# GpSimd takes over the wait for landed additions, the expert tiles lie in two lists, and rectified rows are made between two exponentials

## The chip, the cores and the metric

The kernel runs on one core of one Trainium2 chip. The metric is the device time of one execution in microseconds (us), median of several runs; lower is better. TensorE (PE in the profile) does matrix products and transposes, VectorE (DVE) and ScalarE (ACT) do the elementwise work, GpSimd (POOL) issues the indirect DMAs, SyncE (SP) issues the plain ones.

## What is computed

Three layers over 6250 nodes of 256 features: graph attention (`gnn`), a linear-attention block (`mix`), and a mixture of six experts (`ffn`), of which each node takes two. The change lies wholly in the last of them:

```python
xn = _layernorm(x, axis=-1)
x = x + _L0_gnn_ref(xn, ...) + _L0_mix_ref(xn[None], ...)[0]
x = x + _L0_ffn_ref(_layernorm(x, axis=-1)[None], ...)[0]

def _L0_ffn_ref(features, ...):
    rh = jax.nn.relu(features @ router_w1 + router_b1)
    expert_logits = jax.nn.softmax(rh @ router_w2 + router_b2, axis=-1)
    top_w, top_i = jax.lax.top_k(expert_logits, TOP_K)        # TOP_K = 2, six experts
    routing_weights = jax.nn.softmax(top_w, axis=-1)
    h1 = jax.nn.relu(jnp.einsum('bsd,edh->bseh', features, expert_w1) + expert_b1)
    h2 = jax.nn.relu(jnp.einsum('bseh,ehf->bsef', h1, expert_w2) + expert_b2)
    expert_out = jnp.einsum('bsef,efo->bseo', h2, expert_w3) + expert_b3
    sel = jnp.take_along_axis(expert_out, top_i[:, :, :, None], axis=2)
    return jnp.sum(sel * routing_weights[..., None], axis=2)
```

## The kernel before

Everything below happens in the last block of the kernel, from about 1740 us of the span on. Each engine has its own instruction stream, in program order; semaphores tie them together.

**Router stage.** The 50 row tiles of 125 nodes are taken in `NS` = 5 groups of `SIZES` = (6, 10, 10, 12, 12). For group g, ScalarE makes the normalised rows (`features`, line 2219), TensorE transposes them and runs the router (lines 2303, 2313, 2322) with ScalarE copying in between, and VectorE's `route(g)` takes the logits (line 2074), asks ScalarE for an exponential (line 2276, waits for `d_lm`), picks the two best experts, and after the instruction of line 2088 asks for a second exponential (line 2278, waits for `d_dd`). VectorE doesn't wait for this second one at once: it first counts ranks and comes to it at line 2100 (`a_ee`). ScalarE, though, stands at line 2278 till `d_dd` comes. Only then it makes the rectified attention rows of group g + 2 (`relus`, line 2208), and then goes to `features(g + 1)`. With `route(g)` done (`d_pos`), GpSimd writes each row of the group twice, once into the region of either expert in the DRAM tensor `moe_rows` (line 1951, two indirect DMAs for a row tile, 100 in all).

**List of tiles.** `MT` = 54 tiles of 256 rows are worked through, each with rows of one expert. `table_of(0)` (after group 3's counts) lists the first `FULL` = 20 of them, from the full tiles that the first `EARLY` = 3 groups give each expert. `table_of(1)`, called by VectorE after its tile step 1, lists tiles 20 to 53: the rest of the first list (full tiles of the early groups, expert by expert), then a second list (the further full tiles, expert by expert), then a third (the partly filled tile of each expert). Each is a run of instructions on segments, `SEG` = 18 of them for three lists; the comparison of 34 tiles with 18 segments has 612 elements. From the list VectorE also makes `clear1` and `clear2`: for tile j the count that the semaphore `sent[...]` of tile j - 1 (j - 2) must have reached before tile j may be added. If both tiles belong to one expert no node is in both, and the count is one that was reached long ago; if the expert changed, it is the count that says that the earlier additions have landed in `out`.

**Tile loop.** For tile j SyncE loads the rows (line 1928), TensorE transposes them (line 2349, `row_turn`) and multiplies by three weight matrices (`up` line 2360, `mid` line 2371, `down` line 2384). Its order is up(j+1), mid(j), row_turn(j+2), down(j-1). ScalarE copies and rectifies (lines 2239, 2247, 2256). VectorE's order in its step j is stage1(j+2), stage2(j+1) (copies of the expert's weights and biases), weighed(j-1), stage3(j): the products of tile j - 1 are scaled into the buffer `yo` (line 2171, two halves), then the third weight matrix is copied (line 2145), which `down(j)` needs. `yo` has three buffers, so weighed(j) also waits till the additions of tile j - 3 have landed. Before that `weighed` reads `clear1` and `clear2` from memory into registers (line 2161) and waits on `sent[...]` (this is the wait that moves). GpSimd issues two indirect DMAs a tile that add the rows of `yo` to `out` (line 1971), and in tiles 0 to 8 also the two writes of one more row tile of the last group (line 1951; three of its twelve row tiles were written ahead).

At tile 20 SyncE first fills the ends of the six regions with a blank (line 1919) and waits for it before it loads on.

Of the kernel before, what the change touches and what calls it, by code (L numbers as in the profile page):

```python
# [18 lines left out]
ALU = mybir.AluOpType  # L19
# [114 lines left out]
def gps_kernel(nc, x, src, dst, gW, gWb, ga, gab, Wq, bq, Wk, bk, Wv, bv, Wo, bo, W1, b1, W2, b2,  # L134
# [7 lines left out]
    with ExitStack() as ctx:  # L142
# [1656 lines left out]
        odd6 = take(NX)  # L1799
        SEG = 3 * NX  # L1800
        fulls = take(SEG + NX)
        seg_n, seg_end, seg_off = take(SEG), take(SEG), take(SEG)
        seg_step = take(3, NX)
        cmp_mem = take((MT - FULL) * SEG)
# [88 lines left out]
        with nc.Block() as block:  # L1893
# [37 lines left out]
            def _(g_):  # L1931
                last_node = g_.to_reg(N - 1)
                g_.memset(blank[:, 0:MW - 2], 0.0)
                g_.memset(blank[:, MW - 2:MW - 1].bitcast(I32), N)
# [32 lines left out]
                g_.wait_ge(base_out, 16 * NS)  # L1967
                for j in range(MT):
                    g_.wait_ge(d_y, 2 * j + 2)
                    for s in range(2):  # L1970
                        g_.indirect_dma_start(out=out, out_offset=bass.IndirectOffsetOnAxis(ap=node[:, j % RING3, s:s + 1], axis=0),  # L1971
                                              in_=yo[:, j % 3, s, :], in_offset=None, bounds_check=last_node, oob_is_err=False,
                                              compute_op=ALU.add).then_inc(sent[j % PB3], 16)
                    if AHEAD_OF_ADDS + j < SIZES[g]:
                        write(g, AHEAD_OF_ADDS + j, sent_late)
# [4 lines left out]
            def _(dve):  # L1980
# [13 lines left out]
                dve.wait_ge(z3, 4)  # L1994
                V.memset(seg_step[:, 2, NX - 1:NX], -float((NX - 1) * PACK) + float(PACK // 4)).then_inc(z3, 1)

# [37 lines left out]
                def table_of(k):  # L2034
# [14 lines left out]
                    if k == 1:  # L2049
                        step(V.scalar_tensor_tensor(odd6, whole, -float(MR), count, ALU.mult, ALU.add))  # L2050
                        step(V.scalar_tensor_tensor(fulls[:, SEG:SEG + NX], odd6, 1.0, whole, ALU.min, ALU.add))
                    V.tensor_tensor(seg_off[:, 0:n], fulls[:, 1:1 + n], fulls[:, NX:NX + n], ALU.subtract)
# [63 lines left out]
                regs = [dve.alloc_register(f"expert{i}") for i in range(4)]  # L2116
                clears = [dve.alloc_register(f"clear{i}") for i in range(4)]
                found = [dve.alloc_register(f"found{i}") for i in range(2)]

# [35 lines left out]
                def weighed(j):  # L2155
                    e = expert(j)
                    held = []
                    for back, clear in ((1, clear1), (2, clear2)):
                        if j >= back:
                            k, reg = (j - back) % PB3, clears[2 * (j % 2) + back - 1]  # L2160
                            dve.reg_load(found[back - 1], clear[0:1, j:j + 1])
                            dve.reg_alu(reg, found[back - 1], 0, ALU.max)
                            held.append((sent[k], dve.snap(reg, min_val=sent_rows[k], max_val=landed(j - back))))
                    for other, value in held:
                        dve.wait_ge(other, value)
                    dve.wait_ge(t_d, j + 1)
# [34 lines left out]
            def _(act):  # L2201
# [60 lines left out]
                for g in range(NS):  # L2262
# [12 lines left out]
                    act.wait_ge(d_lm, g + 1)  # L2275
                    A.activation(pe_[0:R, 0:n], lm[0:R, 0:n], ACT.Exp).then_inc(a_pe, 1)
                    act.wait_ge(d_dd, g + 1)
                    A.activation(ee[0:R, 0:n], dd[0:R, 0:n], ACT.Exp).then_inc(a_ee, 1)
                    if g + 2 < NS:
                        relus(g + 2)  # L2280
                row_turned(1)
# [162 lines left out]
```

## Time and profile before

| | us |
|---|---|
| three runs | 2219.26, 2229.14, 2229.53 |
| median | 2229.14 |
| the profiled execution: its time | 2220.27 |
| the profiled execution: its span | 2218.5 |
| TensorE busy in it | 1856.9 (84%) |
| VectorE busy | 1689.0 (76%) |
| ScalarE busy | 1441.6 (65%) |
| GpSimd busy | 1201.3 (54%) |
| router stage and tile loop | about 1740 to 2211 of the span |

A row of a timeline gives the start and the length of an instruction (or of a run of them) in us, its engine, line, operation and operands, and in brackets how long the engine had been idle before it and what ended this. "issue" is idle time that no recorded wait explains. PEclk is the granted clock of TensorE as a share of full speed.

### The profile page before, as it was taken

The numbers are of one execution on the slowest core, as the hardware profiler recorded it, in microseconds if no ns is written. First come the engines' busy times: TensorE is split into PE (matmuls) and PEld (weight loads), VectorE is DVE, ScalarE is ACT, GpSimd is POOL, SyncE is SP. The second block draws the span as 40 slices with busy tenths as digits, with TensorE's granted clock in tenths as the row PEclk, the third lists the DMA queues.
The fourth block names the chain that finished last, engine by engine and source line by source line (L and its number), as shares of the span: only waits on it lengthen the run. The fifth ranks groups of instructions, "written<-read, shape, count | busy, mean of one in ns | idle before, by whom it ended". The sixth has DMA issues, their size and how long they took to land. (4 is left out here: it accounts for less than half of the span.)

```text
span 2218.5 us, 49553 instructions
## 1 busy us (share of the span) xinstructions
PE 1856.9 (84%) x10024; PEld 1491.2 (67%) x10024; DVE 1689.0 (76%) x5423; ACT 1441.6 (65%) x4425; POOL 1201.3 (54%) x1164
## 2 busy tenths in 40 slices
PE   3888857599954999999999999999999556999995
PEld 2444435377743778877878778878877455778884
DVE  7898879877754788888888889888898655455553
ACT  5567558244412889889889889889889663333331
POOL 2010000056565777777777777777774167755553
PEclk9999979599856999999999999999999768999997
DMA  4322101021103444444443444444442454655551
GB/s 144 95 76 60 53 24 52 19 83 49 42 23 84 121 119 119 122 119 117 122 118 111 120 114 117 123 117 117 122 117 69 148 172 136 118 117 89 101 92 26
DMA packets 133895, 215.45 MB, mean 97 GB/s; under 512 B 42813, under 2 KB 89084, under 8 KB 133604
## 3 DMA queue, kind: packets, MB, share of 16 engines
q0 software_dynamic: 61920, 132.16, 24.9%
q1 hardware_dynamic: 67022, 72.68, 10.7%
q10 hardware_dynamic: 4662, 7.46, 1.1%
q8 instruction: 94, 1.54, 0.3%
q14 instruction: 197, 1.61, 0.2%
HBM read 150.28 MB, written 56.51 MB: 93 GB/s over the span
## 5 line engine op out<-in xcount | busy, mean ns | idle before, releaser
L1394 POOL DMA_INDIRECT area<-wh_table,area x788 | 769.9, 977 | 260.2 <-issue 235.0
L1721 PE MATMUL bank<-area 128*126 x1960 | 484.2, 390 | 31.0 <-ACT area L1641 15.3
L1721 PEld LDWEIGHTS bank<-area 128*126 128x126 f32 x1960 | 349.8, 188 | 103.8 <-issue 55.1
L1427 DVE TENSOR_SCALAR area<-iota_row,area 128x126 f32<-128x126 f32 x980 | 355.0, 369 | 24.5 <-ACT area L1594 17.3
L1627 ACT ACTIVATE area<-iota_row,area 128x126 f32<-128x126 f32 x735 | 285.8, 389 | 0.0
L1971 POOL DMA_INDIRECT out_dram<-area x108 | 171.2, 1585 | 134.3 <-DVE area L2171 115.7
L1641 ACT ACTIVATE area<-area 128x126 f32<-128x126 f32 x735 | 237.0, 386 | 0.4
L590 POOL DMA_INDIRECT sorted_slots<-area x112 | 134.9, 1204 | 115.9 <-DVE area L946 85.4
L1580 ACT ACTIVATE area<-bank 125x512 bf16<-125x512 f32 x245 | 145.4, 593 | 79.2 <-DVE area L1441 76.1
L1741 PE MATMUL bank<-area 128*128 128x250 f32 x800 | 189.1, 380 | 6.8 <-ACT area L1648 3.7
L1502 DVE SCALAR_TENSOR_TENSOR acc_mem<-acc_mem,area,bank 125x258 f32 x245 | 117.8, 481 | 97.0 <-PE bank L1709 82.4
L1752 PE MATMUL bank<-area 128*125 128x256 f32 x800 | 188.9, 379 | 0.0
L1697 PE MATMUL bank<-ident,area 128*126 128x128 f32 x980 | 158.1, 284 | 34.8 <-DVE area L1427 34.8
L1741 PEld LDWEIGHTS bank<-area 128*128 128x128 f32 x800 | 154.0, 193 | 27.0 <-ACT area L1648 4.1
L1441 DVE TENSOR_REDUCE area<-bank 125x1 f32<-125x512 f32 x245 | 167.5, 684 | 0.0
L1752 PEld LDWEIGHTS bank<-area 128*125 128x125 f32 x800 | 150.0, 187 | 23.0
L2171 DVE SCALAR_TENSOR_TENSOR area<-bank,area 128x256 f32<-128x256 f32 x108 | 47.5, 480 | 142.8 <-DMA out_dram<-area 74.0
L2247 ACT ACTIVATE area<-bank,area 128x256 f32<-128x256 f32 x108 | 45.3, 470 | 159.7 <-issue 147.2
L583 POOL IOTA acc_mem<- 128x788 f32 x1 | 0.8, 793 | 272.7 <-DVE area L855 272.7
L1951 POOL DMA_INDIRECT moe_rows<-acc_mem,area x100 | 100.4, 1004 | 67.2 <-issue 28.6
L1697 PEld LDWEIGHTS bank<-ident,area 128*126 128x126 f32 x980 | 103.9, 141 | 40.0 <-DVE area L1427 39.7
L2384 PE MATMUL bank<-area 128*128 128x256 f32 x432 | 108.1, 394 | 16.3 <-DVE area L2145 16.3
(417 smaller groups left out, 4050.4 us busy)
## 6 DMA issues: line engine op xcount, KB each, us to landing
area<-moe_rows SPq DMA_DIRECT2D x54, 264.0 KB, 2.9
area<-wh_table,area POOLq DMA_INDIRECT x788
area<-area SPq DMA_DIRECT2D x17, 388.5 KB
wh_table<-area SPq DMA_DIRECT2D x50, 126.5 KB
xn<-in_x_dram SPq DMA_DIRECT2D x25, 250.0 KB
xt_rows<-area SPq DMA_DIRECT2D x50, 125.0 KB, 2.5
area<-xt_rows SPq DMA_DIRECT2D x25, 250.0 KB
x_rows<-area SPq DMA_DIRECT2D x25, 250.0 KB
```

The lines of the kernel that those rows point to most:

```text
L590: g.indirect_dma_start(out=slots[k % 2].rearrange("(a b) -> a b", b=1), out_offset=bass.IndirectOffsetOnAxis(ap=dest[:, j, k:k + 1], axis= ...
L1394: g.indirect_dma_start(out=gath[:, (i + GT) % RS, :], out_offset=None, in_=table, in_offset=bass.IndirectOffsetOnAxis(ap=idx_tab[:, i:i + ...
L1427: ins = V.tensor_scalar(xm[:, b, t, :], iota_row[:, :], rowl[:, j % 10, t:t + 1], fetched(j, D)[:, t:t + 1], ALU.is_equal, ALU.mult)
L1441: V.tensor_reduce(gmax[0:R, b:b + 1], bank[XT[j % 2]][0:R, :], AX.X, ALU.max).then_inc(d_m, 1)
L1580: A.activation(hot[0:R, b, :], bank[XT[j % 2]][0:R, :], ACT.Sign).then_inc(a_hot, 1)
L1627: last = A.activation(dist[:, t, :], iota_row[:, :], ACT.Abs, bias=rowl[:, j % 10, t:t + 1], scale=-1.0)
L1641: last = A.activation(sm[:, b, t, :], dist[:, t, :], ACT.Exp, bias=e3[:, b, t:t + 1], scale=-1.0e12)
L1697: last = T.transpose(bank[XT[j % 2]][0:RW, t * L:(t + 1) * L], xm[:, b, t, :], ident[:, :])
L1721: last = T.matmul(bank[US[b]][0:RW, 0:WROW], sm[:, b, t, :], gath[:, bass.ds(place + t, 1), 0:WROW].rearrange("p a w -> p (a w)"), start=( ...
L1741: last = T.matmul(bank[HB[p % 2]][:, i * CH:(i + 1) * CH], w_1[:, k, f * 128:(f + 1) * 128], x1T[:, k, :], start=(k == 0), stop=(k == 1))
L1752: last = T.matmul(bank[AB][0:R, r * D:(r + 1) * D], hT[:, f, r * R:(r + 1) * R], w_2[:, f, :], start=(f == 0), stop=(f == 7))
L1971: g_.indirect_dma_start(out=out, out_offset=bass.IndirectOffsetOnAxis(ap=node[:, j % RING3, s:s + 1], axis=0), in_=yo[:, j % 3, s, :], in_ ...
```

## The change

1. The reads of `clear1` and `clear2` and the waits on `sent[...]` leave VectorE's `weighed`. GpSimd does them before it issues tile j's additions: it waits for `tabled`, reads both values, waits for `d_y` as before, then waits for the two counts.
2. The tiles from 20 on lie in two lists, not three: the second list has for each expert its further full tiles and its partly filled one (`whole` becomes the number of both). `SEG` is 12, the comparison has 408 elements. The number of tiles is the same.
3. ScalarE makes `relus(g + 2)` after the first exponential of group g and before it waits for the second one, for g = 0, 1, 2.

```diff
--- before.py
+++ after.py
@@ -1797,10 +1797,10 @@
         sel, seen, going = (a.rearrange("p (e t) -> p e t", e=NX) for a in (sel_mem, seen_mem, going_mem))
         blank_i, count_i = take(NX).bitcast(I32), take(NX).bitcast(I32)
         odd6 = take(NX)
-        SEG = 3 * NX
+        SEG = 2 * NX
         fulls = take(SEG + NX)
         seg_n, seg_end, seg_off = take(SEG), take(SEG), take(SEG)
-        seg_step = take(3, NX)
+        seg_step = take(2, NX)
         cmp_mem = take((MT - FULL) * SEG)
         ej_f, both_f = take(MT), take(MT)
         both_i = take(MT).bitcast(I32)
@@ -1930,6 +1930,8 @@
             @block.gpsimd
             def _(g_):
                 last_node = g_.to_reg(N - 1)
+                clears = [g_.alloc_register(f"clear{i}") for i in range(4)]
+                found = [g_.alloc_register(f"found{i}") for i in range(2)]
                 g_.memset(blank[:, 0:MW - 2], 0.0)
                 g_.memset(blank[:, MW - 2:MW - 1].bitcast(I32), N)
                 g_.memset(blank[:, MW - 1:MW], 0.0)
@@ -1966,7 +1968,17 @@
                     write(g, i, sent_late)
                 g_.wait_ge(base_out, 16 * NS)
                 for j in range(MT):
+                    g_.wait_ge(tabled, 1 if j < FULL else 2)
+                    landings = []
+                    for back, clear in ((1, clear1), (2, clear2)):
+                        if j >= back:
+                            k, reg = (j - back) % PB3, clears[2 * (j % 2) + back - 1]
+                            g_.reg_load(found[back - 1], clear[0:1, j:j + 1])
+                            g_.reg_alu(reg, found[back - 1], 0, ALU.max)
+                            landings.append((sent[k], g_.snap(reg, min_val=sent_rows[k], max_val=landed(j - back))))
                     g_.wait_ge(d_y, 2 * j + 2)
+                    for added, value in landings:
+                        g_.wait_ge(added, value)
                     for s in range(2):
                         g_.indirect_dma_start(out=out, out_offset=bass.IndirectOffsetOnAxis(ap=node[:, j % RING3, s:s + 1], axis=0),
                                               in_=yo[:, j % 3, s, :], in_offset=None, bounds_check=last_node, oob_is_err=False,
@@ -1992,7 +2004,7 @@
                 V.memset(going[0:R, :, 0:1], 0.0)
                 V.memset(seg_step[:, :, NX - 1:NX], -float((NX - 1) * (PACK + REG))).then_inc(z3, 1)
                 dve.wait_ge(z3, 4)
-                V.memset(seg_step[:, 2, NX - 1:NX], -float((NX - 1) * PACK) + float(PACK // 4)).then_inc(z3, 1)
+                V.memset(seg_step[:, 1, NX - 1:NX], -float((NX - 1) * PACK) + float(PACK // 4)).then_inc(z3, 1)
 
                 def residual(g):
                     for c in pairs[g]:
@@ -2048,7 +2060,7 @@
                     step(V.tensor_copy(whole, count_i))
                     if k == 1:
                         step(V.scalar_tensor_tensor(odd6, whole, -float(MR), count, ALU.mult, ALU.add))
-                        step(V.scalar_tensor_tensor(fulls[:, SEG:SEG + NX], odd6, 1.0, whole, ALU.min, ALU.add))
+                        step(V.scalar_tensor_tensor(whole, odd6, 1.0, whole, ALU.min, ALU.add))
                     V.tensor_tensor(seg_off[:, 0:n], fulls[:, 1:1 + n], fulls[:, NX:NX + n], ALU.subtract)
                     step(V.tensor_tensor(seg_n[:, 0:n], fulls[:, NX:NX + n], fulls[:, 0:n], ALU.subtract))
                     V.scalar_tensor_tensor(seg_off[:, 0:n], seg_off[:, 0:n], float(MR), step_n, ALU.mult, ALU.add)
@@ -2114,8 +2126,6 @@
                     V.tensor_copy(posi[0:R, :, f:f + n], posf3[0:R, :, 0:n]).then_inc(d_pos, 1)
 
                 regs = [dve.alloc_register(f"expert{i}") for i in range(4)]
-                clears = [dve.alloc_register(f"clear{i}") for i in range(4)]
-                found = [dve.alloc_register(f"found{i}") for i in range(2)]
 
                 def expert(j):
                     return dve.snap(regs[j % 4], min_val=0, max_val=NX - 1)
@@ -2154,15 +2164,6 @@
 
                 def weighed(j):
                     e = expert(j)
-                    held = []
-                    for back, clear in ((1, clear1), (2, clear2)):
-                        if j >= back:
-                            k, reg = (j - back) % PB3, clears[2 * (j % 2) + back - 1]
-                            dve.reg_load(found[back - 1], clear[0:1, j:j + 1])
-                            dve.reg_alu(reg, found[back - 1], 0, ALU.max)
-                            held.append((sent[k], dve.snap(reg, min_val=sent_rows[k], max_val=landed(j - back))))
-                    for other, value in held:
-                        dve.wait_ge(other, value)
                     dve.wait_ge(t_d, j + 1)
                     if j >= 3:
                         dve.wait_ge(sent[j % PB3], landed(j - PB3))
@@ -2274,10 +2275,10 @@
                         up(0)
                     act.wait_ge(d_lm, g + 1)
                     A.activation(pe_[0:R, 0:n], lm[0:R, 0:n], ACT.Exp).then_inc(a_pe, 1)
+                    if g + 2 < NS:
+                        relus(g + 2)
                     act.wait_ge(d_dd, g + 1)
                     A.activation(ee[0:R, 0:n], dd[0:R, 0:n], ACT.Exp).then_inc(a_ee, 1)
-                    if g + 2 < NS:
-                        relus(g + 2)
                 row_turned(1)
                 for j in range(MT):
                     if j + 1 < MT:
```

## Rows read from the trace of the kernel before

**Rows 1.** Engines by stretch: busy us (instructions), PEclk, DMA share, GB/s
```profile
2050.00:2100.00 50.00, 50.00 (x250) 43.72 (x249) 29.53 (x102) 18.83 (x45) 29.27 (x20) 1.00 0.58 99
```

**Rows 2.** Waits from 1900 us on: waiter <- releaser: us in total, times, longest
```profile
POOL out_dram L1971 <- DVE area L2171: 113.6, 45, 8.6
DVE area L2171 <- DMA out_dram<-area: 69.7, 22, 8.5
...
PE bank L2384 <- DVE area L2145: 16.3, 8, 4.3
...
PE bank L2349 <- DMA area<-moe_rows: 4.9, 1, 4.9
```

**Rows 3.** Chain that ended last, in order of time: start, us, what
```profile
2077.03 1.74 PE bank L2384 x8
...
2082.66 1.74 PE bank L2384 x8
...
2193.99 1.57 POOL out_dram L1971
2195.87 3.57 DMA out_dram<-area
```

**Rows 4.** Timeline of VectorE, line 2171 at tiles 1, 2, 8 and 13
```profile
1888.22 0.88 DVE L2171 SCALAR_TENSOR_TENSOR area<-bank,area 128x256 f32<-128x256 f32 x2 [0.79 <-DMA out_dram<-area]
...
1895.56 0.88 DVE L2171 SCALAR_TENSOR_TENSOR area<-bank,area 128x256 f32<-128x256 f32 x2 [3.57 <-DMA out_dram<-area]
...
1935.28 0.88 DVE L2171 SCALAR_TENSOR_TENSOR area<-bank,area 128x256 f32<-128x256 f32 x2 [8.49 <-DMA out_dram<-area]
...
1962.86 0.88 DVE L2171 SCALAR_TENSOR_TENSOR area<-bank,area 128x256 f32<-128x256 f32 x2 [1.86 <-PE bank L2384]
```

**Rows 5.** Timeline of TensorE, three places where it waited for VectorE (before down(9) and down(25), and at up(4))
```profile
1887.05 2.58 PE L2360 MATMUL bank<-area 128*128 128x256 f32 x8 [3.92 <-DVE area L2131]
...
1936.54 3.46 PE L2384 MATMUL bank<-area 128*128 128x256 f32 x8 [4.16 <-DVE area L2145]
...
2041.58 2.00 PE L2384 MATMUL bank<-area 128*128 128x256 f32 x8 [0.93 <-DVE area L2145]
```

**Rows 6.** Timeline of GpSimd: first write of group 3; first additions of tiles 0, 3, 7, 44, 53
```profile
1843.59 0.97 POOL L1951 DMA_INDIRECT moe_rows<-acc_mem,area  x1 [3.54 <-DVE area L2114]
...
1881.99 1.93 POOL L1971 DMA_INDIRECT out_dram<-area  x1 [0.30 <-issue]
...
1903.31 1.62 POOL L1971 DMA_INDIRECT out_dram<-area  x1 [0.30 <-issue]
...
1929.34 1.62 POOL L1971 DMA_INDIRECT out_dram<-area  x1 [0.32 <-issue]
...
2147.90 1.57 POOL L1971 DMA_INDIRECT out_dram<-area  x1 [2.21 <-DVE area L2171]
...
2207.43 1.55 POOL L1971 DMA_INDIRECT out_dram<-area  x1 [3.27 <-DVE area L2171]
```

**Rows 7.** Timeline of ScalarE: second exponential of groups 0 and 2, rectified rows of group 3
```profile
1758.42 0.21 ACT L2278 ACTIVATE area<-area 125x6 f32<-125x6 f32 x1 [2.50 <-DVE area L2088]
...
1782.36 4.88 ACT L2208 ACTIVATE acc_mem<-acc_mem,area 125x256 f32<-125x256 f32 x12
...
1806.55 0.21 ACT L2278 ACTIVATE area<-area 125x10 f32<-125x10 f32 x1 [2.80 <-DVE area L2088]
```

**Rows 8.** Timeline of VectorE: use of the second exponential; the comparison of either table
```profile
1784.04 0.17 DVE L2100 TENSOR_SCALAR area<-area 125x10 f32<-125x10 f32 x1
...
1838.92 0.28 DVE L2056 TENSOR_TENSOR area<-area 128x120 f32<-128x120 f32 x1
...
1881.64 0.80 DVE L2056 TENSOR_TENSOR area<-area 128x612 f32<-128x612 f32 x1
```

**Rows 9.** Register reads of line 2161: ns min/median/max, first and last start
```profile
L2161 DVEq TENSOR_LOAD <-area x105: 297/312/803, 1887.1 to 2201.9; - x105
```

**Rows 10.** Additions of line 1971, from the start of an issue to landing
```profile
DMA to landing us min/median/max: 2.7/3.9/5.0
```

## The prediction, made from the kernel before alone

> **What bounds the kernel now.** I first read the engines by stretch. In the middle of the tile loop TensorE is busy for all of 50 us, at its full granted clock, and no other engine for more than 30 [rows 1]. The chain of waits says the same: its products follow each other without a gap, and one tile takes 2082.66 - 2077.03 = 5.63 us, which I call the beat, 5.64 [rows 3]. So what a change can give lies where TensorE stands still. The list of waits has the places: GpSimd waits 113.6 us for VectorE and VectorE 69.7 us for landed additions, but TensorE itself waited for VectorE only 16.3 us in eight places [rows 2]. The difference is cover: after a late `weighed(j-1)` VectorE still has 2 to 3 us in hand before `down(j)` needs its copy. Of the 69.7 us most is therefore worth nothing. Uncovered are the wait before tile 8 (VectorE 8.49 us, TensorE 4.16) [rows 4, 5], two of about 1 us at tiles 25 and 26 (the first is in [rows 5]), and the end. There the last seven tiles (47 to 53) each have another expert than the one before: issue 1.57 us, gap, issue, landing 3.57, VectorE 0.9, issue [rows 3], 6.6 to 7 us a tile and not 5.64. Changes of expert can be counted by VectorE's waits for a DMA: tiles 1, 2, 8, 14, 22, 24, 25, 26, 32, 38, 45 and 47 to 53, 18 in all. In the first nine tiles GpSimd is a second bound: it has two writes beside each tile's two additions, never idles, and takes (1929.34 - 1903.31) / 4 = 6.51 us a tile [rows 6], more than the beat. In the router stage the bound is the round ScalarE, TensorE, ScalarE.
>
> **Rectified rows between the exponentials.** Before the second exponential of groups 0, 1 and 2 ScalarE idles 2.50 to 2.80 us (three waits, 8.0 together) [rows 7]. The rectified rows (4.88 us for twelve) now lie in this gap, so `features` of the next group starts earlier each time: 8.0 less about 0.15 a group for a later restart, 7.6 us for the round and for the first tile of the loop. The price: the second exponential comes about 5 us after the first. VectorE used it at 1784.04 in group 1 [rows 8]; it would be there at about 1784.5, 0.5 us late. VectorE has that to spare: at the end of each group it waits for ScalarE anyway. GpSimd gains less. Its writes of groups 1 and 2 run on without a gap, so it gains the first 2.4 less 0.5, and then the idle 3.54 before group 3 [rows 6] shrinks to 0.3: 1.9 + 3.2 = 5.1 us. Tile 0's additions start at 1876.9, not 1881.99.
>
> **Two lists.** Three instructions on 612 elements take 0.80 us each, on 120 elements 0.28 [rows 8]: 1.06 ns an element, 204 elements fewer, 0.65 us in all. TensorE waits for just this table (3.92 us before up(4)) [rows 5], so it is a gain. Changes of expert fall from 18 to 12: none in the last tiles but that of the filler tile 53. With the wait on GpSimd a change costs little: 1.87 us between the two issues, 3.9 from issue to landing [rows 10] and 0.15 make 5.9, against the beat of 5.64. By itself the second edit is worth 0.65 and some 2 to 4 us at the end.
>
> **The wait on GpSimd.** VectorE is freed. It waits for tile j - 3 only, so the 4.16 us at tile 8 go, and with them what the first products after it lost by a low clock (3.46 and not 1.90 us, 1.56) [rows 5]. TensorE is then up by 7.6 + 0.65 + 5.7 = 14.0 us at tile 9. What GpSimd takes on is r, a time per tile for two reads of memory into registers, two register operations and the extra waits; later tiles hide it, since GpSimd idles 2.21 us before an issue [rows 6], but tiles 1 to 9 don't. No read by GpSimd is in the trace. The nearest rows are VectorE's reads of the same words: 0.312 us median [rows 9], with the register operations 1.1 us when nothing covers them, which is the upper bound of the likely case; the lower is 0, if GpSimd's sequencer reads while the write before it (0.97 us) is still made. With a single read VectorE still stood 0.79 us [rows 4], so reads are covered in part at best; GpSimd's cover of 0.97 us is most of the 1.1, but its sequencer isn't seen to work ahead. I take 0.5, between the two. What is queued behind the new wait on GpSimd: the writes of the last group, which SyncE needs only at tile 20. At the changes 2 and 8 the two writes lie between the issue and the wait (1.6 + 2 x 1.28 + gaps = 4.5 us against 3.9), so nothing is added there.
>
> By the Trainium skill (Perfetto Trace Analysis, DMA Instruction — SWDGE) the sequencer is free to fetch on once such an instruction is in the wait queue. That would hide the reads; yet the rows show a gap of 0.30 us between any two of them, unexplained. By that rule the sum would be its r = 0 case.
>
> So GpSimd starts tile 9 at 1876.9 + 6.7 (tile 0) + 8 x 6.51 + 9r = 1935.7 + 9r (tile 0 as before: issues of 1.93 and 1.57, two writes, four gaps), tile 10 at 3.8 + r more: 1944.5 for r = 0.5. `yo` has three buffers, so `weighed(13)` can't start before 1944.5 + 5.9 = 1950.4. It started at 1962.86 [rows 4]: a gain of 12.4, less than TensorE's 14.0, and the smaller decides. From there the beat holds, as 3.8 + r is below 5.64.
>
> **The rest.** SyncE's load for tile 20 makes TensorE wait 4.9 us [rows 2]: SyncE can send the blanks only after tile 19's load, which waits for VectorE's tile 15, and that came some 1.5 us late as tile 14 was a change. I take 1.0 (0 to 1.5). Tiles 25 and 26: 2.0. End: tiles 44 to 53 took 2207.43 - 2147.90 = 59.5 [rows 6]. After: six beats 33.8, one without a transpose 5.2, one of GpSimd's own 3.8 + 0.5, and 5.9 for the filler tile: 49.2. Gain 10.3. What follows the last issue stays.
>
> Sum: 12.4 + 1.0 + 2.0 + 10.3 = 25.7. With r = 0: 14.0 + 1.5 + 2.0 + 10.8 = 28.3. With r = 1.1 `weighed(13)` comes at 1956.4, gain 6.5, and 6.5 + 0 + 2.0 + 9.7 = 18.2.
>
> **The rivals.**
> Dear reads, r from 1.2 to 1.9. For: between two DMA instructions GpSimd always shows a gap, so its sequencer may not work ahead. Against: VectorE's reads are 0.3. At r = 1.5 the gain at tile 13 is 2.5, at the end 9.3, with the 2.0 some 14: 2215.
> The Trainium skill (DMA: Bandwidth & Descriptors, Latency and other measured facts) gives such a load a floor of about 600 ns. VectorE's 312 ns don't agree; if GpSimd's did, two would be 1.2 us, by that an r of this rival.
>
> The start is eaten. The router stage begins earlier for TensorE, but GpSimd's issues or SyncE's loads keep their time. For: GpSimd gains only 5.1 of 7.6 in any case. Against: its 3.54 us gap is plain. With 7 us less the gain is 18 to 19: 2210.
>
> Slower: GpSimd becomes the bound of every tile. Its own work is 3.72 us a tile; above r = 1.92 it passes the beat. Its last tile then starts at 1876.9 + 6.7 + 52.1 + 44 x 3.72 + 53r = 2099.4 + 53r, which meets today's 2207.43 at r = 2.04. At r = 2.5 it is 24.5 us later: 2254. It would need reads three times as long as VectorE's.
>
> Nothing changes: freed time is lost to more transfers at once, landings rise from 3.9 us towards 5.0 [rows 10] and TensorE waits on `yo` or on row loads. A landing of 5.0 makes a change 7.0 us, still for 12 tiles only, and without changes three buffers allow three beats: under 10 us lost, so this takes more than one mishap. About 2226.
>
> **How the numbers follow.** The profiled execution had 2220.27; with 25.7 less it is 2194.6. The four executions lie at two levels, 2219 to 2220 and 2229, and the median of 2229.14 is of the upper, which gives 2203.4. I say 2199.0, between them. Chances: the forecast (r to 1.1) 0.68, with the gain from 18 to 28; dear reads 0.12, a third of it within 0.5%; start eaten 0.10; slower 0.05; nothing 0.05. From 2219 less 28 and the level's spread the range starts at 2187; above it takes in the smaller gains to 15 us from the upper level, 2214. A difference below 0.5%, 11 us, can't be told from none here. So faster 0.87, within 0.08, slower 0.05.
>
> **What would show it.** ScalarE's line 2278 without idle time in groups 0 to 2. GpSimd's gap before line 1971 in tiles 3 to 7: 0.30 + r; its beat there 7.0 us. VectorE's line 2171 with short DMA waits only in tiles 10 to 14. No wait of 4 us before down(9). Last tiles at 5.64. Wrong it would be if GpSimd's issues after tile 12 follow each other with no idle time, or if TensorE stands longer than before in front of up(4) or row_turn(20).

## The result, and the profile after

The changed kernel takes 2193.95 us (median of four executions, 2192.44 to 2203.05) against 2224.20 (four, 2218.12 to 2229.53). The ratio is 0.9879, with a 95% interval of 0.9847 to 0.9911. That is 27 us less (the two medians lie 30 us apart), and more than the 11 us below which the prediction would have called it no difference. The forecast was 2199.0, with a range from 2187 to 2214. The profiled execution had 2192.44 us with a span of 2190.5, 28.0 less than the span of before.

The page of the changed kernel: busy times, and the chain that ended last by engine.

```profile
PE 1854.1 (85%) x10024; PEld 1491.2 (68%) x10024; DVE 1690.2 (77%) x5423; ACT 1442.9 (66%) x4425; POOL 1202.5 (55%) x1164
...
PE 16%; issue 2%; DVE 1%; ACT 1%; DMA 0%; POOL 0%; SPq 0%; DVEq 0%; POOLq 0%; ACTq 0%
```

No engine's busy time changed by more than 2.8 us. What changed is who waits. Waits of the changed kernel from 1880 us on (waiter <- releaser: us in total, times, longest):

```profile
DVE area L2172 <- PE bank L2385: 112.9, 52, 7.2
POOL out_dram L1983 <- DVE area L2172: 80.7, 39, 7.2
POOL out_dram L1983 <- issue: 27.3, 62, 3.4
...
PE bank L2361 <- DVE area L2141: 4.1, 1, 4.1
...
POOL out_dram L1983 <- DMA out_dram<-area: 3.9, 5, 2.7
...
PE bank L2350 <- DMA area<-moe_rows: 3.3, 1, 3.3
...
PE bank L2385 <- DVE area L2155: 1.4, 1, 1.4
```

Against [rows 2]: VectorE's 69.7 us behind landed additions are gone. GpSimd waits for them in VectorE's place, with 3.9 us put down to a landing and part of the 27.3 us of "issue". TensorE's eight waits for the copies before `down` (line 2145 of before, 16.3 us) are one, at the very end. What stays are the table (4.1) and the load of tile 20 (3.3).

TensorE's timeline of the changed kernel has the three waits. Below it, from GpSimd's timeline, the first additions of tiles 44 and 53:

```profile
1879.66 3.78 PE L2361 MATMUL bank<-area 128*128 128x256 f32 x8 [4.15 <-DVE area L2141]
1973.47 1.12 PE L2350 MATMUL bank<-ident,area 128*128 128x128 f32 x4 [3.26 <-DMA area<-moe_rows]
2173.29 2.00 PE L2385 MATMUL bank<-area 128*128 128x256 f32 x8 [1.42 <-DVE area L2155]
```

```profile
2130.74 1.57 POOL L1983 DMA_INDIRECT out_dram<-area  x1 [2.21 <-DVE area L2172]
...
2179.77 1.55 POOL L1983 DMA_INDIRECT out_dram<-area  x1 [2.72 <-DMA out_dram<-area]
```

Tiles 44 to 53 take 49.03 us where they took 59.53 [rows 6].

For comparing many kernels one origin is needed. The code ahead of this block is the same in all, yet the block begins anywhere from 1737 to 1750 us of the span. So the table counts from the start of ScalarE's first normalised row of the block (line 2220 of the changed kernel, the column "block starts"). The next columns are starts of `weighed(j)` on VectorE, in us after that origin, and the end of the span, each from one profiled execution. Before and after begin together, so their difference of 28.1 is that of the spans.

| kernel | block starts | w(0) | w(3) | w(8) | w(13) | w(16) | w(17) | w(44) | w(53) | end |
|---|---|---|---|---|---|---|---|---|---|---|
| before | 1744.6 | 133.1 | 156.0 | 190.7 | 218.2 | 235.2 | 247.3 | 402.1 | 461.7 | 473.9 |
| changed | 1744.7 | 125.4 | 149.0 | 177.2 | 205.3 | 222.2 | 232.8 | 384.9 | 430.7 | 445.8 |
| wait_only | 1742.7 | 134.7 | 157.6 | 185.8 | 214.0 | 230.9 | 243.7 | 396.4 | 442.6 | 463.4 |
| lists_only | 1742.1 | 132.1 | 154.2 | 189.3 | 217.1 | 234.0 | 246.1 | 398.2 | 447.4 | 459.6 |
| relus_only | 1746.9 | 125.1 | 148.9 | 184.0 | 212.8 | 229.7 | 242.9 | 397.5 | 456.5 | 468.7 |
| no_lists | 1742.3 | 125.6 | 149.3 | 177.5 | 205.7 | 222.6 | 232.9 | 385.2 | 431.1 | 451.3 |
| no_wait_move | 1737.4 | 125.4 | 149.0 | 183.8 | 212.8 | 229.7 | 243.0 | 396.3 | 445.7 | 457.8 |
| reads12 | 1750.0 | 124.9 | 148.6 | 176.7 | 204.9 | 221.8 | 234.5 | 386.9 | 432.8 | 448.0 |
| reads3_live | 1746.6 | 125.2 | 147.2 | 175.4 | 203.5 | 220.4 | 231.7 | 384.4 | 430.3 | 445.2 |
| reads6_live | 1747.0 | 125.7 | 149.1 | 177.3 | 205.4 | 222.3 | 235.1 | 387.5 | 433.4 | 448.5 |
| blanks_early | 1750.4 | 125.9 | 148.0 | 176.1 | 204.3 | 221.2 | 226.8 | 378.9 | 424.7 | 440.0 |
| table_early | 1747.7 | 125.4 | 142.2 | 171.5 | 201.4 | 218.3 | 231.2 | 383.7 | 429.6 | 444.8 |
| both_early | 1749.7 | 125.3 | 142.1 | 171.2 | 201.2 | 218.2 | 223.8 | 375.9 | 421.7 | 436.8 |

The step from w(16) to w(17) holds TensorE's wait for the rows of tile 20. In the kernels that leave that load where it was it takes 10.3 to 13.3 us where a beat is 5.64. The changed kernel and its repeat (reads12) have 10.6 and 12.7, so some 2 us of this are no property of a kernel.

### The profile page after: what moved, and what is told of

Read it like the earlier page. It is cut to its first block and busy times, and to the rows that moved or that the text cites. A ratio compares the mean times of both kernels' runs of the same rounds, so it can differ in the third digit from the quotient of the medians.

```text
span 2190.5 us, 49554 instructions
## 1 busy us (share of the span) xinstructions
PE 1854.1 (85%) x10024; PEld 1491.2 (68%) x10024; DVE 1690.2 (77%) x5423; ACT 1442.9 (66%) x4425; POOL 1202.5 (55%) x1164
```

## The experiments

### Each part alone

Part 1 alone, GpSimd's wait (`weighed` on VectorE loses its reads and waits as in the change):

```diff
+                    g_.wait_ge(tabled, 1 if j < FULL else 2)
+                    # reads of clear1, clear2 as in the change
                     g_.wait_ge(d_y, 2 * j + 2)
+                    for added, value in landings:
+                        g_.wait_ge(added, value)
```

> Only the wait on landed additions moves to GpSimd; three lists and the late rectified rows stay. Theory (GpSimd's reads are covered by the write that is being made, and a change of expert costs GpSimd 5.9 us against a beat of 5.64): TensorE loses no 4.16 us before down(9), 1 us twice at tiles 25 and 26, and 1.5 us less at tile 20; the last seven tiles go at 5.9 each. 5.7 + 1.7 + 2 + 6.6 = 16 us, span 2202.5 against 2218.5. Rival 1 (the gain of the whole change comes from fewer changes of expert and the early rectified rows): under 5 us, span over 2213. Rival 2 (GpSimd's reads cost): its gap before line 1971's first issue in tiles 3 to 7 is 0.8 to 1.4 us and not 0.30.

Measured: ratio 0.9930 (0.9909 to 0.9950), median 2209.04. By the ratio that is 15.6 us (11 to 20), near the 16 expected. From the block's start its one profile ends at 463.4, 10.5 us before the kernel before. Its first tile came 1.6 us late, though nothing ahead of it is edited; without that it would be 12. The loop gained what was said: no wait before down(9), w(53) 19 us earlier. The last stretch gave some back. GpSimd's first additions in it:

```profile
2176.48 1.55 POOL L1983 DMA_INDIRECT out_dram<-area  x1 [3.21 <-issue]
...
2182.79 1.68 POOL L1983 DMA_INDIRECT out_dram<-area  x1 [2.89 <-DVE area L2172]
...
2189.21 1.55 POOL L1983 DMA_INDIRECT out_dram<-area  x1 [2.88 <-issue]
...
2195.37 1.55 POOL L1983 DMA_INDIRECT out_dram<-area  x1 [2.75 <-issue]
```

They are 6.2 to 6.4 us apart where every tile has another expert than the one before, not 5.9. Over tiles 44 to 53 that makes 2195.37 - 2140.25 = 55.1 us: better than 59.5, worse than the 49.0 that parts 1 and 2 give together. In tiles 45 and 47 to 53 of this run GpSimd's addition starts 0.74 us after the landing that it waited for. In the kernel before, with VectorE's two halves of `weighed` between them, it is 1.30 in the same tiles. So moving the wait saves 0.56 us of each such change.

Part 2 alone, two lists:

```diff
-        SEG = 3 * NX
+        SEG = 2 * NX
...
-                        step(V.scalar_tensor_tensor(fulls[:, SEG:SEG + NX], odd6, 1.0, whole, ALU.min, ALU.add))
+                        step(V.scalar_tensor_tensor(whole, odd6, 1.0, whole, ALU.min, ALU.add))
```

> Only two lists for three; VectorE still waits for landed additions. Theory: the end gains 9 us (six of seven changes of expert gone), tiles 25 and 26 gain 2 us as two changes in a row are gone; the 4.16 us before down(9) stay. The table is 0.65 us shorter, of which little arrives. Span about 2207, gain 11 to 12. Rival (each change of expert costs TensorE, 18 to 12): gain of a third of 28 or less evenly spread. Rival (the list is worth only the table): under 1.5 us.

Measured: 0.9951 (0.9932 to 0.9969), median 2210.29, end at 459.6: 14.3 us less, of which 1.0 was there at the first tile. The end gives most: w(44) to w(53) fell from 59.6 to 49.2. The wait before down(9) remains, as TensorE's timeline shows:

```profile
1932.63 3.70 PE L2384 MATMUL bank<-area 128*128 128x256 f32 x8 [5.36 <-DVE area L2145]
```

Part 3 alone, the rectified rows:

```diff
                     A.activation(pe_[0:R, 0:n], lm[0:R, 0:n], ACT.Exp).then_inc(a_pe, 1)
+                    if g + 2 < NS:
+                        relus(g + 2)
                     act.wait_ge(d_dd, g + 1)
                     A.activation(ee[0:R, 0:n], dd[0:R, 0:n], ACT.Exp).then_inc(a_ee, 1)
-                    if g + 2 < NS:
-                        relus(g + 2)
```

> Only the rectified rows between the exponentials. Theory: TensorE starts the tile loop 7.6 us earlier, but GpSimd only 6.1 us earlier, and VectorE's wait before tile 8 is for GpSimd's tile 7, so that 1.5 us are given back there: gain 6.1, span 2212.4, and the wait before down(9) grows from 4.2 to about 5.5 us. Rival (ScalarE's round carries all): gain 7.6 and the wait before down(9) unchanged. Rival (start eaten): gain under 2.

Measured: 0.9969 (0.9950 to 0.9988), median 2218.50. The first tile is 8.0 us earlier, w(13) still 5.4, the end 5.2. So without the moved wait 2.6 us of the start are handed back before tile 13. The first 0.9 is gone by w(3), where up(4) is slower; this is taken up below. The rest goes where VectorE waits for landings, since GpSimd's additions of tiles 0 and 7 come only 6.3 and 6.6 us earlier, and in the clock behind the wait before down(9). TensorE's timeline:

```profile
1932.18 3.78 PE L2384 MATMUL bank<-area 128*128 128x256 f32 x8 [4.61 <-DVE area L2145]
```

The wait is 4.61 us where it was 4.16, and the product behind it takes 3.78 where it took 3.46 [rows 5]: the granted clock in this product was 0.50 where it was 0.57.

The three alone make 10.5 + 14.3 + 5.2 = 30.0 us by their profiles, the whole 28.1. By the ratios they make 15.6 + 10.9 + 6.9 = 33 us against 27, each of the three uncertain by 4 to 5. So the parts add up roughly, and neither sum shows more than that.

### The change without one part

Without part 2 (waits moved, rectified rows moved, three lists):

> The changed kernel with three lists again (parts 1 and 3 alone). Times are counted from ScalarE's first normalised row to the end of the span, which leaves out what differs earlier: before 473.9, changed 445.8. Theory after wait_only: a change of expert costs GpSimd 6.2 to 6.5 us when several follow each other (0.7 us pass between the end of its wait and its next issue), so tiles 47 to 53 are bound by GpSimd and the end is 5 to 6 us later: 451 to 452. Rival (my forecast's 5.9 a change): 3 us. Rival (lists worth only the table): under 1.

Measured: 0.9904 (0.9871 to 0.9936), median 2198.40. Its w(44) and w(53) are those of the changed kernel to 0.4 us, and the end, at 451.3, is 5.5 later. Once GpSimd does the waiting, the third list costs nothing but a tail behind VectorE's last tile.

Without part 1 (two lists, rectified rows moved, VectorE waits as before):

> The changed kernel with the wait on landed additions back on VectorE (parts 2 and 3 alone). From ScalarE's first normalised row to the end: theory 454 to 455 (lists_only 459.6 less the 5.2 of relus_only): VectorE's wait before tile 8 comes back with a wait of TensorE before down(9) of over 4 us and a low clock after it, and of the 7.7 us of the earlier start about 2 are lost there. Rival (with few changes of expert it doesn't matter who waits): 446 to 448.

Measured: 0.9918 (0.9887 to 0.9948), median 2201.70, end at 457.8, 12.0 us after the changed kernel and some 3 more than expected. It is level at w(3), 6.6 behind at w(8), 7.5 at w(13), and 10.2 behind at w(17). The last 2.7 of these are in TensorE's wait for tile 20, 5.76 us there and 3.26 in the changed kernel. Behind it a wait of 0.88 us before down(25) remains, and w(44) is 11.4 behind. The two waits that make most of it:

```profile
1922.40 3.78 PE L2384 MATMUL bank<-area 128*128 128x256 f32 x8 [4.36 <-DVE area L2145]
...
1975.93 1.11 PE L2349 MATMUL bank<-ident,area 128*128 128x128 f32 x4 [5.76 <-DMA area<-moe_rows]
```

### What reads cost on GpSimd

In the changed kernel the gap ahead of line 1983 was 0.30 us in tiles 3 to 7, as before, though a tile has two reads. Timeline of GpSimd, first additions of tiles 3 and 7 with the writes ahead of them, then all reads of line 1976 (duration ns min/median/max, first and last start):

```profile
1894.54 1.22 POOL L1953 DMA_INDIRECT moe_rows<-acc_mem,area  x1 [0.30 <-issue]
1896.07 1.62 POOL L1983 DMA_INDIRECT out_dram<-area  x1 [0.31 <-issue]
...
1920.83 0.98 POOL L1953 DMA_INDIRECT moe_rows<-acc_mem,area  x1 [0.30 <-issue]
1922.11 1.62 POOL L1983 DMA_INDIRECT out_dram<-area  x1 [0.30 <-DMA out_dram<-area]
```

```profile
L1976 POOLq TENSOR_LOAD <-area x105: 282/288/671, 1873.3 to 2173.4; - x105
```

So either the reads are hidden altogether, or something that took their time before is gone. More reads tell these apart. They were put behind the first read of a tile (3, 6 or 16 of them; the values take part in the count, so that they have to be made):

```diff
                             g_.reg_load(found[back - 1], clear[0:1, j:j + 1])
+                            for _i in range(3 if back == 1 else 0):     # 6, 16
+                                g_.reg_load(again, clear[0:1, j:j + 1])
+                                g_.reg_alu(found[0], found[0], again, ALU.max)
```

The first attempt had twelve reads whose value nobody used.

> The changed kernel with twelve more reads of a word into a register on GpSimd in each tile but the first, before it waits for d_y (14 in all; results unchanged). This puts the price of the forecast's slower rival on the chip. Theory (a read is 0.29 us and a gap of 0.04, made while the instruction before it still runs, and only what passes this cover is paid): the reads take 4.7 us a tile, GpSimd's tile is 1.57 + 0.3 + 4.8 = 6.7 us or more, above the beat of 5.63, and it becomes the bound of all 54 tiles: tile 53 starts at about 1876 + 6.6 + 8 x 10 + 44 x 6.8 = 2262, span about 2273, 80 us slower than the changed kernel. Rival (reads run wholly beside the DMA instructions and waits): no change, span 2190.5. Rival (nothing is covered, and the two present reads are cheap for another reason): 3.72 + 4.7 = 8.4 us a tile, span over 2330.

Measured: 0.9895 (0.9854 to 0.9936), end at 448.0. Nothing follows for the reads: the trace has none of the twelve (105 reads, as in the changed kernel), so the program was that of the changed kernel. It serves as its repeat, and shows by how much the same kernel varies: 2.2 us at the end, 2.1 of them in the step of tile 17.

> The changed kernel with three more reads a tile on GpSimd, each with a maximum of registers that uses it, so that none can be dropped (the twelve of reads12 had no user and the trace has none of them). Theory: a read with its register operation takes 0.45 us; GpSimd's sequencer starts them with the DMA instruction before and pays what passes its end, and 0.7 us after the last: in tiles 3 to 7 the gap before the first addition is about 1.9 us and not 0.3, a tile 8.1 us and not 6.5, tile 13 of VectorE's line 2172 comes 8 us later, and from first normalised row to end it is 455, 9 longer. This is the forecast's dear reads. Rival (reads cost nothing however many): 446 to 448. Rival (yo's three buffers don't bind): tiles at 8.1 but the end as before.

> As reads3_live with six. Theory: 3.5 us of reads a tile; tiles 3 to 7 at 9.4 us; later tiles 1.87 + 3.5 + 0.7 = 6.1 us and so all bound by GpSimd: from first normalised row to end about 490, 45 longer than the changed kernel and slower than the kernel before (474). This is the forecast's slower rival at its price. Rival (the beat stays with TensorE): 460.

Measured: three more reads 0.9881 (0.9840 to 0.9922), end at 445.2; six more 0.9865 (0.9812 to 0.9918), end at 448.5. Both expectations of a cost are wrong. With eight reads a tile GpSimd's timeline still has the gap of 0.30 us:

```profile
1902.24 0.99 POOL L1954 DMA_INDIRECT moe_rows<-acc_mem,area  x1 [0.30 <-DMA out_dram<-area]
1903.53 0.98 POOL L1954 DMA_INDIRECT moe_rows<-acc_mem,area  x1 [0.30 <-issue]
1904.82 1.75 POOL L1987 DMA_INDIRECT out_dram<-area  x1 [0.30 <-issue]
1906.87 1.76 POOL L1987 DMA_INDIRECT out_dram<-area  x1 [0.30 <-issue]
```

and its added reads began at 1876.5, for an addition that started at 1884.99:

```profile
L1979 POOLq TENSOR_LOAD <-area x318: 282/285/991, 1876.5 to 2181.2; - x159
```

Eight reads with their register operations are over 3 us of sequencer time, more than any one instruction beside them, the longest being 1.8. So GpSimd's sequencer runs ahead of its DMA instructions by several, not by one. The times in the changed kernel say the same: the first read for tile 8 is at 1917.33 and its first addition at 1929.02, with seven DMA instructions started in between. The Trainium skill (Perfetto Trace Analysis, DMA Instruction — SWDGE) says that the sequencer may fetch on once such an instruction is in the wait queue; the trace agrees.

> As reads3_live with sixteen further reads. Eight reads a tile (reads6_live) cost GpSimd nothing, since its sequencer reads for tile j + 1 while several DMA instructions before it still wait or run. Theory now: the sequencer is an engine of its own, and reads cost only when they alone fill a tile: 18 reads and their register operations are 0.36 to 0.4 us each, 6.5 to 7.2 us, above the beat of 5.63; then the sequencer is the bound of all tiles: from first normalised row to end 131 + 53 x 7 + 17 = 500 to 520, against 446 to 448. Rival (it hides any number, as it runs ahead without limit): 446 to 448; that can't be, as it would have to be done with tile 53's reads in time. Rival (cover ends with the instructions that are queued): about 30 longer.

Measured in one execution: 2354.64 us, end at 604.7, 131 us behind the kernel before. More than the 500 to 520 expected. Here is the slower case of the prediction, and it can be read in the chain that ended last (start, us, what), between two tiles:

```profile
2230.89 0.71 issue
2231.61 0.86 POOL out_dram L1987
2232.50 0.28 POOLq L1979
...
2239.07 0.29 POOLq L1977
2239.38 0.07 POOLq L1981
2239.46 0.05 issue
2239.50 0.04 POOLq L1985
2239.55 0.71 issue
2240.26 0.53 POOL out_dram L1987
```

Of 8.65 us from one tile's first issue to the next, the sequencer needs 0.89 until its first read, 7.05 for 18 reads with what belongs to them (0.39 a read), and 0.71 between the end of its last wait and the issue. That is a bound of its own. If its two parts hold for other numbers of reads, it is 1.60 + 0.39 n for n reads and reaches the beat of 5.64 at about ten; for the change's two it is 2.4. These are estimates from this run; none with nine to seventeen reads was made. It also says why eight cost nothing: 4.7 us is still below both the beat and the 6.5 of the first nine tiles.

### What is late next

TensorE has two long waits left in the changed kernel. One edit was made for each. The six blanks that SyncE sends at tile 20 went one by one before the row loads of tiles 6 to 11:

```diff
-                    if j == FULL:
+                    if 6 <= j < 6 + NX:
+                        e = j - 6
                         sp.wait_ge(tabled, 2)
-                        for e in range(NX):
-                            sp.reg_load(ends[e % 2], blank_i[0:1, e:e + 1])
-                            ...
+                        sp.reg_load(ends[e % 2], blank_i[0:1, e:e + 1])
+                        ...
+                    if j == FULL:
                         sp.wait_ge(blanked, 16 * (NX + 1))
```

> The changed kernel; SyncE sends the six blanks one by one before the row loads of tiles 6 to 11 and not all six before that of tile 20. Theory: TensorE's wait for the rows of tile 20 (3.3 us and a low clock after it, 5.0 in all in the changed kernel, up to 7 in others) is gone: line 2172 of tiles 16 and 17 are 5.63 us apart, and from first normalised row to end it is 440 to 441, against 446 to 448. Rival (a blank a tile makes the row loads late): TensorE waits for row_turn in tiles 6 to 12 and nothing is gained.

Measured: 0.9836 (0.9796 to 0.9876), median 2188.44. From w(16) to w(17) it takes 5.6 us, one beat: the wait is gone, and the end is at 440.0, as expected.

The second table was made before `weighed(0)` rather than behind it:

```diff
+                    if j == 1:
+                        table_of(1)
                     if j > 0:
                         weighed(j - 1)
-                    if j == 1:
-                        table_of(1)
```

> The changed kernel; VectorE makes the second table one instruction group earlier, before weighed(0) and not after stage3(1), where it idled 5.8 us. Theory: TensorE's 4.15 us before up(4) and the low clock after it are gone, 6.4 us at tile 3; but GpSimd starts no earlier and takes 6.5 us a tile till tile 8, so that the three buffers of yo give back some: VectorE's line 2172 of tile 13 is 4.7 us earlier, 200.6 after the first normalised row, and the end 441. Rival (GpSimd isn't near the bound): 6.4 arrives, end 439.5. Rival (the idle time was needed): under 2.

Measured: 0.9861 (0.9824 to 0.9897), median 2192.45, end at 444.8 and not 441. Against the changed kernel w(3) is 6.8 us earlier, w(13) 3.9, the end 1.0. So most of it is lost again, in two places. The step of tile 17 took 12.9 us and not 10.6; that is within what the changed kernel's own repeat shows (12.7), and against this repeat the end is 3.2 us earlier. And between w(3) and w(13) TensorE has new waits, before down(9), down(10):

```profile
1933.60 2.00 PE L2385 MATMUL bank<-area 128*128 128x256 f32 x8 [0.48 <-DVE area L2155]
1940.55 2.00 PE L2385 MATMUL bank<-area 128*128 128x256 f32 x8 [0.84 <-DVE area L2155]
```

GpSimd's pace (6.56 us a tile in tiles 3 to 7) is now the limit that was forecast for the changed kernel and wasn't met there: `yo` isn't free. VectorE waits for landed additions again, in tiles 8 to 12 (from its list of waits; the changed kernel's has no such row):

```profile
DVE area L2172 <- DMA out_dram<-area: 14.2, 5, 3.0
```

Both edits together:

> Both of the two changes before. Theory: they add, as they lie in different tiles: from first normalised row to end 436, ratio to the kernel before about 0.983. Rival: the earlier tiles bring the blanks into the stretch where GpSimd is the bound, and only one of the two arrives: 441.

Measured: 0.9836 (0.9807 to 0.9865), median 2185.82, end at 436.8, 9.0 us ahead of the changed kernel and 37 ahead of the kernel before. It is the best version by the time from the block's start, though its ratio can't be told from that of blanks_early. The same small waits stand before `down`, as in

```profile
1942.24 2.00 PE L2386 MATMUL bank<-area 128*128 128x256 f32 x8 [0.85 <-DVE area L2156]
```

## Why the prediction was right, and where its steps were off

**The place of the bound, right.** It said that most of VectorE's 69.7 us is worth nothing, and that the gain lies in the start, tile 8, tiles 25 and 26 and the end. 69.7 us of waits vanished and 28.0 came out. From the table: w(13) 12.9 earlier, the step of tile 17 another 1.5, the beats up to tile 23 0.4, tiles 24 to 44 2.3, tiles 44 to 53 10.5, and 0.3 behind the last issue, together 27.9. The forecast had 12.4 + 1.0 + 2.0 + 10.3 = 25.7.

**Rectified rows, right up to the first tile.** w(0) came 7.7 us earlier (forecast 7.6). ScalarE's second exponential has no idle time ahead of it, and VectorE waited 0.27 us for it in group 1 (0.5 forecast). GpSimd's first addition came at 1875.90, 1.0 us before the forecast.

```profile
1780.90 0.19 ACT L2281 ACTIVATE area<-area 125x10 f32<-125x10 f32 x1
```

```profile
1781.13 0.17 DVE L2112 TENSOR_SCALAR area<-area 125x10 f32<-125x10 f32 x1 [0.27 <-ACT area L2281]
```

**The table, a term that arrives in part.** The three instructions on the whole comparison fell from 0.80 to 0.58 us:

```profile
1874.17 0.58 DVE L2068 TENSOR_TENSOR area<-area 128x408 f32<-128x408 f32 x1
```

That is the 0.65 in all that was priced. But TensorE's wait for it was 4.15 us against 3.92. From the comparison to up(4) it took 5.49 us against 5.41, as small steps of VectorE behind the comparison took longer. The other kernels show how far one profile can be trusted here: with three lists the wait is 3.92 to 4.18 us (before, wait_only, relus_only, no_lists), with two lists 3.30 to 4.15 (eight kernels). On average that is some 0.4 us less, and nothing of it in the changed kernel and its repeat. The step that failed is that instructions which are 0.65 us shorter end the wait 0.65 us earlier.

**The clock at up(4), a cost that the sum put at nothing.** up(4) took 3.78 us where it had taken 2.58 [rows 5]. TensorE by stretch: us busy (instructions), granted clock, DMA share, GB/s; its wait, and up(4):

```profile
1875.00:1879.66 4.66, 0.52 (x3) 0.78 0.43 89
1879.66:1883.50 3.84, 3.83 (x9) 0.50 0.55 109
```

The clock was at the lower of its two levels, 1.2 GHz, through the whole of up(4). This comes with the rectified rows and not with the table: up(4) in lists_only, then in relus_only:

```profile
1883.01 2.00 PE L2360 MATMUL bank<-area 128*128 128x256 f32 x8 [3.30 <-DVE area L2131]
...
1881.60 3.78 PE L2360 MATMUL bank<-area 128*128 128x256 f32 x8 [4.18 <-DVE area L2131]
```

All kernels with the earlier rectified rows and this wait take 3.57 to 3.78 us for it, the three without them 2.00 to 2.66. The prediction priced the low clock behind the wait at tile 8, and none behind this one. So w(3) was 7.0 us ahead and not 7.6 + 0.65 = 8.25. Why the clock falls sooner when the loop starts earlier isn't shown.

**The reads on GpSimd, wrong: r is 0, not 0.5.** The prediction took a value between its ends because the sequencer "isn't seen to work ahead". The reads lie up to 11.7 us before their use, eight a tile leave no mark, and eighteen show the round of the sequencer. The fixed gap of 0.30 us that spoke for a dear read has nothing to do with reads. The citation that was weighed there gave the right case.

**Two misses that cancel.** By the sum, r = 0 makes the gain at tile 13 TensorE's 14.0. It was 12.9, near the 12.4 that stood there for r = 0.5, but by another mechanism; that these two agree is luck. TensorE had 7.0 at w(3) and gained 5.95 between w(3) and w(13) (5.7 forecast: the wait and the clock at tile 8), 12.9 together. GpSimd wasn't the limit: VectorE has no wait for a landing in the changed kernel. table_early shows how near it is: start w(3) 6.8 us sooner, and by w(13) 2.9 of them are given back.

**Tile 20, 1.6 and not 1.0, in part by luck.** The mechanism is there: counted back from w(16), SyncE sends the load of tile 19 8.45 us ahead and not 6.98, so that the blanks behind it start 1.5 us or more sooner. How much of this TensorE gets differs between executions. The load of tile 20 is sent 0.60 us after the last blank has landed (in the changed kernel, wait_only, no_lists and reads3_live, where the trace has this landing), and that blank took 3.65, 5.05, 3.4 and 3.5 us. TensorE's wait is 3.26 us in the changed kernel and 4.78 in its repeat. Over the seven kernels with the moved wait and the blanks at tile 20 it is 4.1 on average (one profile each), over the four without the moved wait 5.3, so some 1.2 us are the change's. What makes a blank land later isn't shown. That the blanks are the cause of the wait is shown: spread, they leave a plain beat.

**The end, right, with a term that was too small.** 49.03 us against 49.2. A change of expert on GpSimd was priced at 5.9 = 1.87 + 3.9 + 0.15. The chain of the changed kernel at the filler tile has its parts (start, us, what):

```profile
2175.49 3.54 DMA out_dram<-area
2179.02 0.03 POOLq L1981
2179.05 0.71 issue
2179.77 1.55 POOL out_dram L1983
```

1.87 us between the two issues (from 2173.62), 3.54 until the landing, and then 0.75, not 0.15, until the next issue starts: 6.15. In wait_only, tiles 46 to 53 have (2195.37 - 2151.53) / 7 = 6.26 on average (wait_only's expectation took 5.9, and this is where its time was missed). With two lists only a few changes stand on the path, and the term cost little. Nor was the filler tile the only change there: tile 50 has another expert than 49 and took 6.33 us, and the next two took 4.49 and 3.91. The prediction had a beat of 5.64, 5.2 and 4.3 for these three, 0.4 more in all. At tile 8, where it had a change cost nothing, GpSimd idled 0.82 us and not 0.30.

**The level, half right.** 25.7 off the profiled 2220.27 gave 2194.6, and the profiled execution after had 2192.44. The 2199.0 came from a median of 2229.14 taken as the upper of two levels. The 40 further executions of the kernel before, beside the experiments, don't show two levels: they lie from 2213.6 to 2232.5 with no gap above 1.6 us, and their medians are 2221.5 to 2224.1. The median of three was a high draw, and the profiled execution was the better base.

**The rivals.** Dear reads fell with reads3_live and reads6_live. The start eaten is real where VectorE waits (relus_only hands 2.6 of 8.0 us back by tile 13); in the whole change 0.7 us of it is lost by w(3), and nothing behind. The slower case is a real mechanism, reads16_live has it, but it starts above eight reads a tile (by the estimate at about ten), not at two. Nothing changed fell: the landings of the changed kernel are those of [rows 10], but for the longest.

```profile
DMA to landing us min/median/max: 2.7/3.9/5.2
```

**The signs.** ScalarE's second exponential without idle time, no wait before down(9) and the last tiles at the beat (tiles 44 to 49 at 5.63 us) came as named. GpSimd's gap was 0.30 + r with r = 0, and its pace in tiles 3 to 7 was 6.51 us and not 7.0. VectorE's short waits for landings in tiles 10 to 14 did not come. One sign of being wrong did: TensorE stood 0.23 us longer before up(4). It pointed at the failed step, but the difference is no more than repeats of this wait show.

## What to carry to other kernels

Move a wait for a landed DMA to the engine that issues the next DMA, if that engine has idle time each round: the engine between, which has products to serve, is then bound by what it computes alone. Here the issuing engine's register reads cost nothing up to eight a round, and by the estimate up to the number n at which 1.60 + 0.39 n us fill the round. Price a stall by what stands behind it: a long one also costs the clock of the products that follow, in some versions of a kernel and not in others (up(4): 2.0 to 3.8 us). A term of half a microsecond can't be read from one pair of profiles. Before adding up gains at the start of a pipeline, check which other engine sets a pace there, since it takes back what exceeds it (table_early: 6.8 us became 3.9 in ten tiles).

## What the runs showed of the hardware that was not expected

GpSimd's sequencer goes on past several indirect DMAs: eight register reads of 0.28 us with their operations leave the gap between two DMA instructions at 0.30 us, in tiles that follow each other without idle time. Its own round becomes the bound at 18 reads: 8.65 us a tile.

Between the landing that GpSimd waits for against a register, or the end of this wait, and the start of the DMA behind it lie 0.71 to 0.76 us, in all the kernels where this wait ends last. Between VectorE's last instruction and the DMA that waited for it lie 0.28 us in most tiles, in the changed kernel too, and between two queued DMA instructions 0.30. Whether the longer time comes from the register or from the landing wasn't separated.

TensorE's wait for the rows of tile 20 lies between 2.8 and 5.8 us over the kernels that send the blanks at tile 20, reads16_live apart, and differs by 1.5 between two executions of one program (3.26 and, in reads12, 4.78). Between the changed kernel and wait_only it differs by 1.50 us, of which the landing of the last blank makes 1.40. What makes this landing vary wasn't settled.
